# The last feed-forward of a two-layer transformer: the last chunk's shared tiles placed behind the routed blocks, and the last routing work placed in front of the first Silu

## The reference, cut to what matters

```python
scores = sigmoid(xt @ gate_w.T)                      # 2048 tokens, 8 experts
top_scores, top_idx = top_k(scores, 2)
top_scores = top_scores / (sum(top_scores) + 1e-20) * 2.5
h = xt @ w1[e]; u = xt @ w3[e]; y = (silu(h) * u) @ w2[e]    # hidden width 176
routed = sum over the two chosen experts of y * its score
shared = (silu(xt @ sw1) * (xt @ sw3)) @ sw2         # hidden width 176, every token
x = x + tanh(g_ffn[1]) * (routed + shared)
```

## Time and profile before

| what | value |
|---|---|
| median of 3 runs | 1598.17 us (1591.24 to 1600.37) |
| the profiled execution: its time | 1597.57 us |
| its span | 1595.8 us |
| TensorE busy over the span | 1367.8 us (86%) |
| `routed_ffn` in it: front | 1439.36 to 1484.38 us from the span's start |
| blocks | 1484.38 to 1571.69 us |
| tail | 1571.69 to 1595.8 us |

### The profile page before, as it was taken

How to read it: one execution, slowest core, us unless ns; L and a number is a source line. 1 busy time by engine, 2 the same in 40 slices (tenths; PEclk the granted TensorE clock), 3 DMA queues, 4 the chain that set the end, 5 groups by cost and what they waited for, 6 DMA issues and landing times. The chain is left out here.

```text
span 1595.8 us, 39932 instructions
## 1 busy us (share of the span) xinstructions
PE 1367.8 (86%) x11222; PEld 1125.3 (71%) x11222; DVE 1221.6 (77%) x4778; ACT 1044.1 (65%) x3349; POOL 854.1 (54%) x1333
## 2 busy tenths in 40 slices
PE   0379999999999999999994988799956998988893
PEld 0378888888898888898983445577745777764672
DVE  5589999999999999999985865466638667755565
ACT  4578888888878888878873443455537675763452
POOL 0676676666666667667651177344442444544242
PEclk9999999999999999999996999899988999998997
DMA  8394499710000000000001165344432222101345
GB/s 318 108 274 103 112 255 253 152 39 0 0 0 0 0 0 0 0 0 0 1 1 60 55 201 165 115 124 124 126 94 94 81 76 74 55 28 54 101 125 195
DMA packets 144671, 142.19 MB, mean 89 GB/s; under 512 B 65969, under 2 KB 125169, under 8 KB 143154
## 3 DMA queue, kind: packets, MB, share of 16 engines
q1 hardware_dynamic: 134290, 112.49, 26.1%
q0 software_dynamic: 10272, 28.39, 4.9%
HBM read 76.77 MB, written 77.80 MB: 97 GB/s over the span
## 5 line engine op out<-in xcount | busy, mean ns | idle before, releaser
L679 ACT ACTIVATE prob<-bS,ntop 128x128 f32<-128x128 f32 x512 | 186.7, 420 | 4.6 <-DVE ntop L485 4.4
L580 POOL TENSOR_TENSOR rs<-ve,half 128x6 f32<-128x6 f32 x128 | 178.1, 1392 | 0.0
L663 ACT COPY pT<-bP 128x512 f32<-128x512 f32 x128 | 75.6, 591 | 143.9 <-PE bP L342 143.9
L588 POOL TENSOR_SCALAR kv<-kv,rs,nb 128x128 f32<-128x128 f32 x256 | 150.9, 596 | 27.4 <-POOL nb L583 27.4
L462 DVE SCALAR_TENSOR_TENSOR qn<-qn,mv,rs 128x128 f32<-128x128 f32 x512 | 154.2, 361 | 6.1 <-POOL rs L580 4.5
L333 PE MATMUL bS<-kT,qT 128*128 128x128 f32 x1024 | 137.0, 277 | 11.5 <-ACT prob L679 11.5
L577 POOL TENSOR_TENSOR ve<-mv,eps 128x6 f32<-128x6 f32 x128 | 35.2, 275 | 197.4 <-DVE mv L455 197.4
L309 PE MATMUL bq<-w,xq 128*128 128x256 f16 x1024 | 133.6, 274 | 4.2 <-DVE xq L434 4.2
L650 ACT ACTIVATE qT<-bqT,vecs 128x256 f32<-128x256 f32 x256 | 134.8, 594 | 3.1 <-PE bqT L293 3.0
L333 PEld LDWEIGHTS bS<-kT,qT 128*128 128x128 f32 x1024 | 125.0, 192 | 14.9 <-issue 13.7
L367 PE MATMUL bY<-wproj,catq 128*128 128x256 f16 x1024 | 132.7, 273 | 0.8 <-DVE catq L505 0.8
(11 more groups left out here) (372 smaller groups left out, 4059.2 us busy)
## 6 DMA issues: line engine op xcount, KB each, us to landing
by_slot<-zeros SPq DMA_DIRECT2D x5, 4096.0 KB, 25.3
f_xblk<-by_slot SPq DMA_DIRECT2D x79, 132.0 KB, 2.1
by_slot<-zeros SPq DMA_DIRECT2D x1, 10112.0 KB, 36.3
l_back<-by_pick SPq DMA_DIRECT2D x16, 512.0 KB, 3.5
f_wstage<-by_expert SPq DMA_DIRECT2D x16, 480.0 KB, 3.5
l_piece<-by_expert SPq DMA_DIRECT2D x16, 352.0 KB, 3.0
f_xblk<-by_slot SPq DMA_DIRECT2D x39, 130.0 KB, 2.1
wo_stage<-in_wproj SPq DMA_DIRECT2D x8, 512.0 KB, 4.4
```

Source lines behind the costliest of these rows:

```text
L580: nc.gpsimd.tensor_tensor(rs[:, t, :], ve[:], r["half"][:, 0:6], ALU.pow).then_inc(rs_ready, 1)
L588: done = nc.gpsimd.tensor_scalar(key, key, rs[:, t, 4 + j:5 + j], nb[:, t, j:j + 1], ALU.mult, ALU.add)
L679: done = nc.scalar.activation(prob[:, t, h, :], bS[:, h, :], ACT.Exp, bias=ntop[:, t, h:h + 1], accum_out=total[:, t, h:h + 1])
```

## The change

Three things are moved; every matmul, activation and vector instruction of the stage is kept, save that VectorE gets one more wait per batch in the tail.

- The front has six tiles (chunks 0 to 2) in place of eight. TensorE enters the blocks when three chunks are added.
- The fourth chunk's two tiles run behind the blocks: on TensorE behind `y_taken` of the last block, on ScalarE behind its last block copy, on VectorE behind its last block step and in front of the final adds. `add_shared(LAST)` stands in the tail after the final adds of four batches; the batches 12 to 15 wait for it.
- The routing steps stand earlier. On ScalarE `act_norm`, `act_high` and `act_ex` come in front of the first Silu. On VectorE `dve_low`, `dve_scores` and `dve_pick` come in front of the first `f_hid`, `dve_nth` after `f_hid` 0, `dve_place` after `f_hid` 1, `own` after `f_low` 2 and `dve_share` after `f_low` 3. On TensorE `pe_turn` stands behind `up(0)`, `pe_logits` behind `up(1)`, `pe_ranks` behind `down_tile(0)`.

```diff
+    FRONT = LAST * NS
 @block.tensor
-            for n in range(STEPS):
-                up(n)
-                if n == 4:
-                    router.pe_ranks(pe, LAST, bh[1])
-                if n >= 2:
-                    down_tile(n - 2)
-                if n == 1:
-                    router.pe_turn(pe, LAST, 1, bh[0][:])
-                if n == 2:
-                    router.pe_logits(pe, LAST, 1, bh[1])
-            down_tile(STEPS - 2)
-            down_tile(STEPS - 1)
-            pe.wait_ge(s["added"], NC)
+            def tiles(first, end):
+                for n in range(first, end):
+                    up(n)
+                    if n == 0:
+                        router.pe_turn(pe, LAST, 1, bh[0][:])
+                    if n == 1:
+                        router.pe_logits(pe, LAST, 1, bh[1])
+                    if n >= first + 2:
+                        down_tile(n - 2)
+                    if n == 2:
+                        router.pe_ranks(pe, LAST, bh[1])
+                down_tile(end - 2)
+                down_tile(end - 1)
+
+            tiles(0, FRONT)
+            pe.wait_ge(s["added"], LAST)
...
+            pe.wait_ge(s["y_taken"], NBLK)
+            tiles(FRONT, STEPS)
 @block.scalar
+            router.act_norm(act, LAST, 1)
+            router.act_high(act, LAST, 1, bh[0][:])
+            router.act_ex(act, LAST, 1, bh[1])
+            tiles(0, FRONT)
...
+            tiles(FRONT, STEPS)
 @block.vector
             router.dve_moments(dve, LAST, 1)
+            router.dve_low(dve, LAST, 1, bh[0][:])
+            router.dve_scores(dve, LAST)
+            router.dve_pick(dve, LAST)
+            for n in range(FRONT):
+                hidden(n)
+                if n == 0:
+                    router.dve_nth(dve, LAST)
+                if n == 1:
+                    router.dve_place(dve, LAST, bh[1])
+                if n % NS == 1 and n > NS:
+                    add_shared(n // NS - 1)
+                rest(n)
+                if n == 2:
+                    own()
+                if n == 3:
+                    router.dve_share(dve, LAST)
+            add_shared(LAST - 1)
...
+            for n in range(FRONT, STEPS):
+                hidden(n)
+                rest(n)
             for b in range(B):
+                if b == CH:
+                    add_shared(LAST)
+                dve.wait_ge(s["added"], NC if b >= LAST * CH else LAST)
                 for k in range(K):
```

More of the change, by code:

```diff
@@ L1675, in _, with tiles @@
                     go_down(i - 3, at_experts[i - 3])
+            pe.wait_ge(s["y_taken"], NBLK)
+            tiles(FRONT, STEPS)
         @block.scalar
         def _(act):
[L1679 to L1695, removed]
+            def tiles(first, end):
+                for n in range(first, end + 1):
+                    if n < end:
+                        t = n % 2
+                        reach(act, s["hidden"], n - 1)
+                        act.wait_ge(s["g"], n + 1)
+                        nc.scalar.activation(act_g[:, t, :], bg[t][:], ACT.Silu, scale=1.0 / WS).then_inc(s["silu"], 1)
+                    if n > first:
+                        t = (n - 1) % 2
+                        reach(act, s["downed"], n - 2)
+                        act.wait_ge(s["hidden"], n)
+                        nc.scalar.activation(high[:, t, :], hid[:, t, :], ACT.Copy).then_inc(s["whole"], 1)
+            router.act_norm(act, LAST, 1)
+            router.act_high(act, LAST, 1, bh[0][:])
+            router.act_ex(act, LAST, 1, bh[1])
+            tiles(0, FRONT)
             for i in range(NBLK + 3):
@@ L1755, in add_shared, with hidden @@
                 done.then_inc(s["added"], 1)
-            router.dve_moments(dve, LAST, 1)
-            for n in range(STEPS):
+            def hidden(n):
                 t = n % 2
@@ L1764, in _, with rest @@
                                                op0=ALU.mult, op1=ALU.mult).then_inc(s["hidden"], 1)
[L1765 to L1778, removed]
+            def rest(n):
+                t = n % 2
                 reach(dve, s["downed"], n - 1)
@@ L1781, in _ @@
                 nc.vector.tensor_tensor(low[:, t, :], hid[:, t, :], high[:, t, :], ALU.subtract).then_inc(s["rest"], 1)
-            add_shared(NC - 1)
+            router.dve_moments(dve, LAST, 1)
+            router.dve_low(dve, LAST, 1, bh[0][:])
[15 more added lines that the diff above has]
+            add_shared(LAST - 1)
             def match(n):
```

## The result

The changed kernel takes 1589.54 us (median of 17 runs, 1585.62 to 1597.86), the kernel before 1596.38 us (17 runs). The ratio is 0.9961, 95% interval 0.9945 to 0.9977: 6.2 us faster, between 3.7 and 8.8, inside the half per cent that was counted as no change. The forecast was 1593.5 us, 4.1 us less than before.

What follows compares the result with a forecast made beforehand. The prediction took TensorE to bound the last stage's blocks and VectorE's queue to be the tail's path. Front −6.2, blocks 0 and tail +2.1 gave −4.1 us, from 1597.57 to 1593.5 us, range 1589 to 1599.

Steps and rivals of the forecast that it cites:

- The front, −6.2 us forecast: Last stage before its blocks: two tiles and two table loads fewer, new pause before the first Silu; end 1478.0, not 1484.2.
- The upper bound: Front: with three falls of the clock its last add ends at 1479.5 us, a gain of 4.7.
- Rival 1: Front: the pauses don't lower the clock; gain 9.2 us, sum −7.1, time 1590.5; 15%.
- Rival 3: Front: the clock stays at 1.2 GHz from the new pause on; 8.7 us later, sum +4.6, time 1602.2; 6%.
- The blocks, 0: Blocks of the last stage: their 87.3 us stay as they are, with rows and block loads ready in time.
- the cover: Start of the blocks: first block load issued at 1469.5, before the first block at 1478; called 8 us thick.
- The tail, +2.1 us forecast: Behind the blocks: final adds begin 0.5 us later and `add_shared(3)` adds 1.57 us in VectorE's row.
- T+7.4: Tail: the last tile's steps end 7.4 us after T, the last block's `y_taken`, against the load's T+6.9.
- the added waits: Tail: one more VectorE wait per batch, taken as 0, at most 0.08 us lost 16 times: 1.3.
- Rival 2: Tail: loads, not VectorE, pace the final adds, so the moved work is hidden whole; −6.2 us, time 1591.4; 7%.
- Rival 4: Tail: TensorE's clock is down behind the blocks, final adds begin 5.7 us late; sum +1.1, time 1598.7; 7%.
- The page's rule on the table load: First Silu in the front: 1.28 us load plus 1.38 drain, making it 1.4 later, result 1594.9; not used.

Runs made afterwards that it cites:

- own_late: The changed kernel with `own` behind `f_low` 3 in place of `f_low` 2 and `dve_share` in front of the tail's first `f_hid`; ratio 0.9964 to the kernel before.
- after_again: The changed kernel once more, unchanged; ratio 0.9965 to the kernel before.
- warm: The changed kernel with extra matmuls whose result nobody reads in TensorE's four pauses of the front; ratio 0.9950 to the kernel before.
- pool_add: The changed kernel with `add_shared(3)` taken from VectorE and done by ScalarE and GpSimd; ratio 0.9980 to the kernel before.
- no_last: The changed kernel without the last chunk's two tiles, `add_shared(3)` and the added wait per batch; ratio 0.9951 to the kernel before.
- tail_only: The kernel before with only the last chunk's two tiles moved behind the blocks, the routing left at its old place; ratio 0.9971 to the kernel before.
- act_swap: The changed kernel with `f_high` 6 in front of Silu 7 in ScalarE's tail order; ratio 0.9972 to the kernel before.

## Why the prediction was right

**The front, −6.2 us forecast.** Measured −8.0 between the first two profiles (0.5 of it because the first `up` left the half clock sooner) and −5.8 between the repeats (44.88 to 39.08). The steps held: the first Silu 9.2 us after the front's start (9.8 forecast), rows ready after 16.9 (17.3), the new pause 2.27 (2.25), the second 2.97 and 2.98 behind `own()` (3.2), own_late shows that it was `own()`. The number of falls was the open term. The forecast took a fall behind the first and the second pause (38.6); after_again had both (39.08), the first profile only one (37.06, where the hand schedule, the engines' lists side by side, says 37.2), and warm none (35.42, hand schedule 35.5). So the steps were right, and the fall behind the second pause is a matter of the execution: of the five profiles with this front, two have it. That the measured front lies near the forecast's is in this much luck. The upper bound was too low: it came from falls of about 1.5 us each, and pool_add's second fall cost 2.9, for a front of 40.47 where three falls were to give 40.1. Rival 1, no fall at all, is out, since the clock fell behind the first pause in all five. Rival 3's ground against it, that the clock comes back within 4 us, didn't hold in pool_add, where it stayed down for nearly 6 us of TensorE's work; it did come back.

**The blocks, 0.** Right: 86.95 and 86.93 in place of 87.31 and 87.09. The 88.10 and 88.40 of no_last and pool_add, with the same blocks, have a fall of the clock in the first of them, which the forecast left out. That the block loads stay hidden was right for the change. But the cover was less than the 8 us in the prediction, which counts to the issue of the load: in tail_only the first block is turned 2.2 us behind the issue, so of the 6.5 us between the issue (1463.49) and the first turn (1470.02) some 4.3 were spare. With the routing where it was, tail_only waits 3.43 us for the load.

**The tail, +2.1 us forecast.** Measured +2.7 (mean of 26.93 and 26.96 against that of 24.11 and 24.39). The step that failed is "`f_hid` 7, `f_high` 7, `f_low` 7 and the hand-overs: T+7.4": I worked the tail out along one tile's chain and not along ScalarE's list, where `f_high` 6 stands behind Silu 7. act_swap takes 0.52 of the missing 0.75 us away. The 1.57 for `add_shared(3)` in VectorE's row was right (1.57, from 1568.79 to 1570.36 in the trace), and the added waits cost nothing (no_last). Rival 2, a tail paced by the loads, is out: the tail with the work behind the blocks is 2.7 us longer than without it, and in pool_add, where the 32 adds take 16.87 us in place of the change's 16.40 with `add_shared(3)` among them, it grows by 0.5. Rival 4 is out as well: from 1557 to 1566 the clock was 1.00.

**The sum, −4.1 us.** The stage gives −3.4 to −5.5 in the change's two profiles, −3.8 on the mean of the five with this front and these blocks, and the timed ratio −6.2 (−3.7 to −8.8). The forecast lies within both ranges. Whether the 1 to 2 us between them are scatter or lie elsewhere stays open: start times of the stage scatter by 8.5 us from execution to execution, which hides it. The time of 1589.54 us is some 4 below the forecast: 1.2 because the kernel before measured 1596.38 where the forecast started from 1597.57, and 2.7 because the medians lie 6.8 apart and not 4.1. By the time alone rival 1 (1590.5) and rival 2 (1591.4) fit better; it is the traces that rule them out.

**The page's rule on the table load.** The first Silu came 1.29 us after the start of its table load (1440.90 to 1442.19), and in all fourteen profiles the Silu behind Exp comes 1.29 or 1.30 after it. By the Trainium skill, "ScalarE: Activation LUTs", What ACT_TABLE_LOAD costs, it would come 2.66 us after the load's start; the traces don't agree with that, and the prediction was right to leave it out.

## What to carry to other kernels

Work moved into another engine's waiting time is free only as far as the queue that ends that wait isn't touched: here the matmuls fill a wait in the tail, but one vector step (1.57 us) and a later first add (1.05, half of it by one queue order) cost 2.7 us of the 4 to 8 gained in the front. Write each engine's list out in program order for the new place; following one tile's chain misses what stands ahead in the queue. And where a stage starts with loads, count the chain that feeds them (here 12.8 us from the row numbers to the first load): moving compute out of the front without moving that chain forward left TensorE waiting 3.43 us for the first block. And where the clock can fall, one profile is one draw: the same front took 37.1 to 40.5 us.

## What the hardware showed beyond that

In the fronts, some pauses of TensorE drop the clock to 1.2 GHz behind them in every profile and some only in a part of them. Behind those of 2.25 to 2.28 us it fell in all ten profiles that have one. Behind those of 2.97 to 2.99 us it fell in three of six: the clock was 1.00 behind it in one execution of the change and 0.56 in another, which was worth 1.3 us, and in pool_add it stayed down for nearly 6 us of TensorE's work, which was worth 2.9. Behind the 1.75 us in front of the blocks it fell in four of ten, and behind those of 1.84 us in none of eight. The traces don't show what decides it. Filling the pauses with unread matmuls kept the clock at 1.00 behind the first `up` and shortened the front to 35.42 us, in one profile. A GpSimd instruction of 2.63 us held one VectorE add for 2.08 us, though the two worked on different batches of x.
